# Field products on one core: two eight-pair pieces stored by partition halves, and other cuts in the head's loads

## The reference

```
vid = jnp.einsum('bfd,de->bfe', x, W)
idx_i, idx_j = jnp.triu_indices(32, k=1)
return x[:, idx_i, :] * vid[:, idx_j, :]        # (4096, 496, 64)
```

## Time and profile before

| what | value |
|---|---|
| median of 3 runs | 1284.18 us (1284.15 to 1284.27) |
| the profiled execution | 1284.16 us |
| its span | 1282.8 us |
| PE busy | 189.0 us (15%) |
| DVE busy | 1080.0 us (84%) |
| POOL busy | 0.2 us, 4 instructions |
| DMA moved | 553.70 MB, mean 432 GB/s |

### The profile page before, as it was taken

One profiled execution on the slowest core, in us unless ns is written; L12 is line 12 of the kernel. 1 busy time (PEld: TensorE's weight loads), 2 busy tenths in 40 slices (PEclk: granted clock), 3 DMA queues, 4 the chain that ended last, 5 costly groups with the idle time before them and its releaser, 6 DMA issues. The chain is left out here.

```text
span 1282.8 us, 1256 instructions
## 1 busy us (share of the span) xinstructions
PE 189.0 (15%) x256; PEld 73.3 (6%) x256; DVE 1080.0 (84%) x273; POOL 0.2 (0%) x4
## 2 busy tenths in 40 slices
PE   2012110302112030300020121103030030301100
PEld 1000000100000010100010000001010010100000
DVE  6589989988897989998027989989988899899980
POOL 0000000000000000000000000000000000000000
PEclk8555565655555565655565555656555565655655
DMA  9999999999999999999999999999999999999999
GB/s 403 438 427 430 443 427 433 445 429 425 439 440 429 431 431 440 430 425 445 423 419 438 428 431 438 436 432 432 442 431 436 426 436 435 427 443 433 433 423 409
DMA packets 11810, 553.70 MB, mean 432 GB/s; under 512 B 1312, under 2 KB 1312, under 8 KB 1312
## 3 DMA queue, kind: packets, MB, share of 16 engines
q1 hardware_dynamic: 6048, 277.38, 50.1%
q10 hardware_dynamic: 5760, 276.30, 49.9%
HBM read 33.59 MB, written 520.09 MB: 432 GB/s over the span
## 5 line engine op out<-in xcount | busy, mean ns | idle before, releaser
L296 DVE TENSOR_TENSOR mem<-mem,vid 128x1024 f32<-128x1024 f32 (+11 forms) x270 | 1079.4, 4068 | 161.2 <-DMA out_dram<-mem 113.0
L319 PE MATMUL vid<-mem,w 128*128 x256 | 189.0, 907 | 1005.6 <-PEq L317 1005.6
L319 PEld LDWEIGHTS vid<-mem,w 128*128 128x128 f32 x256 | 73.3, 300 | 1120.5 <-issue 1120.5
L226 DVE COPY w<-mem 64x64 f32<-64x64 f32 x2 | 0.4, 190 | 5.2 <-DMA mem<-in_r_x_dram 5.2
L223 DVE MEMSET w<- 128x128 f32 x1 | 0.2, 165 | 0.8 <-PEq L344 0.8
L344 POOL MEMSET const-bfloat16-1.0<- 128x1 bf16 x1 | 0.1, 101 | 0.0
L344 POOL MEMSET const-uint8-127<- 128x1 uint8 x1 | 0.1, 101 | 0.0
L344 POOL MEMSET const-float32-0.0<- 128x1 f32 x1 | 0.1, 98 | 0.2 <-issue 0.2
L344 POOL MEMSET const-float32-1.0<- 128x1 f32 x1 | 0.1, 98 | 0.0
## 6 DMA issues: line engine op xcount, KB each, us to landing
out_dram<-mem SPq DMA_DIRECT2D x9, 7680.0 KB, 23.3
out_dram<-mem ACTq DMA_DIRECT2D x3, 7680.0 KB, 23.1
out_dram<-mem SPq DMA_DIRECT2D x3, 7168.0 KB, 21.6
out_dram<-mem ACTq DMA_DIRECT2D x3, 5120.0 KB, 17.3
out_dram<-mem ACTq DMA_DIRECT2D x2, 7168.0 KB, 22.6
out_dram<-mem ACTq DMA_DIRECT2D x2, 6656.0 KB, 21.4
out_dram<-mem SPq DMA_DIRECT2D x2, 6656.0 KB, 19.9
out_dram<-mem ACTq DMA_DIRECT2D x3, 4096.0 KB, 17.5
```

The lines of the kernel that those rows point to most:

```text
L226: lambda: nc.vector.tensor_copy(w2[half, half], mem[half, place + F, :D]),
L296: lambda: nc.vector.tensor_tensor(o, left, right, ALU.mult),
L319: last = nc.tensor.matmul(vid[:, b : b + BANK, :], lhsT=w2[:, :], rhs=xt(b), start=True, stop=True)
```

## The change

Four edits. (1) The three pieces of the head's load have 128, 78 and 18 fields in place of 128, 70 and 26. As the first store waits for the piece before the last, it waits for 8 fields more. (2) Slot 1 of 109 pairs becomes two slots of 8 and 101 pairs, and slot 36 of 128 pairs becomes two of 120 and 8. There are now 76 slots, and the switch from ScalarE's to SyncE's queue is at 39, so that it stands between the same pairs. (3) The two slots of 8 pairs, numbers 1 and 38, are stored in two transfers by partition halves. One half of 64 partitions goes from ScalarE's queue as before. The other goes from GpSimd's queue, with an access pattern on the DRAM side whose leading dimension is 8 (8 groups of 8 rows, each group followed by a row's room that is left empty, so that the pattern doesn't merge). For slot 1 GpSimd has partitions 0 to 63, for slot 38 partitions 64 to 127. (4) GpSimd's transfers also wait for the head's last load.

```
-    (0, [(96, 224), (26, 96), (0, 26)]),
+    (0, [(96, 224), (18, 96), (0, 18)]),
...
-STRETCHES = [37]
+STRETCHES = [39]
+SHIFTS = {1: 0, 38: 1}
...
-    (80, 256), (109, 336), (83, 240, 16), ...
+    (80, 256), (8, 336), (101, 344), (83, 240, 16), ...
...
-    (120, 312), (128, 48), (128, 176), (128, 304), (128, 32), (128, 160), (128, 304), (104, 256), (85, 360),
+    (120, 312), (128, 48), (128, 176), (128, 304), (128, 32), (128, 160), (120, 304), (8, 424), (104, 256), (85, 360),
...
+HALVES = P // 2
-BLOCKS = [0, *accumulate(P * row(n) for n, *_ in SLOTS)]
+BLOCKS = [0, *accumulate((P + 8 * (slot in SHIFTS)) * n for slot, (n, *_) in enumerate(SLOTS))]
...
-    sp, act, dve = (Queue(engine, behind) for engine in (nc.sync, nc.scalar, nc.vector))
+    sp, act, dve, pool = (Queue(engine, behind) for engine in (nc.sync, nc.scalar, nc.vector, nc.gpsimd))
...
     hold = load(0)
+    first_loads = hold
...
-        rows = out[BLOCKS[slot] : BLOCKS[slot + 1], :].rearrange("(p u) c -> p u c", p=P)
-        transfer(rows[:, : end - begin, :], mem[:, units[0] : units[1], :], units, True, needs, act if slot < STRETCHES[0] else sp)
+        queue = act if slot < STRETCHES[0] else sp
+        block = out[BLOCKS[slot] : BLOCKS[slot + 1], :]
+        if slot not in SHIFTS:
+            transfer(block.rearrange("(p u) c -> p u c", p=P), mem[:, units[0] : units[1], :], units, True, needs, queue)
+            return
+        apart, size = (HALVES + 8) * (end - begin), end - begin
+        one, other = (slice(h * HALVES, (h + 1) * HALVES) for h in (SHIFTS[slot], 1 - SHIFTS[slot]))
+        groups = block[:apart, :].rearrange("(g p u) c -> g p (u c)", g=8, u=size)[:, :8, :]
+        rest = block[apart:, :].rearrange("(p u) c -> p u c", p=HALVES)
+        transfer(rest, mem[other, units[0] : units[1], :], units, True, needs, queue)
+        transfer(groups, mem[one, units[0] : units[1], :], units, True, [*needs, (first_loads[-1], 16)], pool)
```

More of the change, by code:

```diff
@@ L46 @@
 STARTS = [0, *accumulate(n for n, *_ in SLOTS)]
-def row(n):
-    return n
-BLOCKS = [0, *accumulate(P * row(n) for n, *_ in SLOTS)]
+HALVES = P // 2
+BLOCKS = [0, *accumulate((P + 8 * (slot in SHIFTS)) * n for slot, (n, *_) in enumerate(SLOTS))]
 BREAKS = sorted({a + s for a, (_, _, *seams) in zip(STARTS, SLOTS) for s in seams} | set(STARTS))
@@ L368, with block @@
     got = r.results[0]["out_0_dram"]
-    got = [got[a:b].reshape(P, -1, C)[:, :n] for a, b, (n, *_) in zip(BLOCKS, BLOCKS[1:], SLOTS)]
+    def block(slot):
+        n, rows = SLOTS[slot][0], got[BLOCKS[slot] : BLOCKS[slot + 1]]
+        if slot not in SHIFTS:
+            return rows.reshape(P, n, C)
+        apart = (HALVES + 8) * n
+        both = [rows[:apart].reshape(8, 9, n, C)[:, :8].reshape(HALVES, n, C), rows[apart:].reshape(HALVES, n, C)]
+        return _np.concatenate(both[::-1] if SHIFTS[slot] else both)
+    got = [block(slot) for slot in range(len(SLOTS))]
     got = _np.concatenate(got, axis=1).reshape(2, D, NT, NP, C)
```

## The result

The changed kernel takes 1287.06 us (median of 8 runs, 1286.48 to 1288.78), the kernel before in the same session 1284.22 us (8 runs, 1283.83 to 1284.95). The ratio is 1.0024, with the interval 1.0013 to 1.0035: slower by 2.8 us. I had forecast 1284.5 us, with a range to 1286.4. The profiled execution took 1287.56 us, its span is 1286.2 us, 3.4 us more than before.

A forecast was written before the change was run, and what follows sets the result against it. The prediction took the always busy DMA engines, at 434.5 GB/s, as the bound. It summed 1284.16 + 0.1 + 0.6 - 0.4 + 0 = 1284.46, forecasting 1284.5 us, with a range from 1282.6 to 1286.4 us.

The forecast's parts named there:

- What bounds the kernel: Whole span: DMA engines busy in every slice; 553.70 MB take 1274.3 of 1282.8 us, only 8.5 us can be won.
- The four parts: Losses: 1.7 us before the first packet, 0.4 at 40 us, 1.4 at 638 us, 1.1 from engines ending apart.
- More transfers, +0.1: ScalarE's and GpSimd's queues: four more transfers with 4 KB rows cost 0 to 0.3 us, taken as +0.1.
- The small halves on ScalarE's queue, +0.6: Slots 1 and 38: 64 partitions through 16 engines cost 0 to +0.6 us each, taken as twice 0.3.
- GpSimd's half, "no such loss": Slots 1 and 38: GpSimd's half, one engine for eight partitions as in a whole store, loses no rate.
- The head, -0.4: Change from loads to stores near 40 us: less overlap of directions gains 0 to 0.9 us, taken as -0.4.
- The lag, 0: From about 45 to 604 us one group of eight engines lags by 1.21 us; cost 0, bounds 0 and +1.2.
- half rate: Rival, small halves on ScalarE's queue: +1.2 in place of +0.6, little head gain, 1285.1 us; chance 0.16.
- GpSimd's transfers on all sixteen engines: Rival, GpSimd's halves of slots 1 and 38: spread over all 16 engines, no lag, 1284.3 us; chance 0.05.
- Both on the same eight: Rival, GpSimd's two transfers: the same eight engines get 8 rows more, 1.21 us, 1285.7 us; chance 0.07.
- A preparation of GpSimd's queue: Rival, before the first load or after the last landing: readying or closing the queue costs 2.9 us, 1287.4 us; chance 0.10.
- "Out of step is better": Rival, first half and end: engine groups meet less, gaining 0.5 us and another 0.4, 1283.2 us; chance 0.14.

The follow-up runs named there:

- head alone: The kernel before with only the head's pieces changed to 128, 78 and 18 fields: 1284.78 us, ratio 1.0005.
- head and cuts: The changed kernel with both slots of 8 pairs stored whole from ScalarE's queue, so edits 1 and 2 only: 1285.29 us, ratio 1.0007.
- one cut: The kernel before with slot 1 cut into 8 and 101 pairs, slot 36 whole, all slots stored whole, head as before: 1284.17 us, ratio 1.0000.
- the old head: Head pieces of 128, 70 and 26 fields as before; the changed kernel with them 1287.14 us, the kernel before with both cuts 1284.42 us.
- the big halves: Slot 2 of 101 pairs stored as two 64-partition halves from ScalarE's queue, against the changed kernel, other slots whole: 1301.62 us, ratio 1.0134.
- the twins: Slot 2 from ScalarE's queue on eight engines, 8 neighbouring partitions an engine in two transfers against 4 in four: 1330.84 and 1308.26 us.
- 34 fields: The kernel before with the head's pieces cut to 128, 62 and 34 fields: 1284.54 us, ratio 1.0002.

## Why the prediction was wrong

The time lay outside the range, 2.6 us above the forecast. By the profiles, on the last engine (landings of the store of slot 6, of the store at 622 us, and the end):

| kernel | slot 6's store | at 622 us | end of span | between | rest |
|---|---|---|---|---|---|
| before | 123.1 | 622.2 | 1282.8 | 499.1 | 660.6 |
| head alone | 122.2 | 622.4 | 1283.1 | 500.2 | 660.7 |
| head and cuts | 122.5 | 622.9 | 1284.5 | 500.4 | 661.6 |
| the full change | 125.0 | 625.4 | 1286.2 | 500.4 | 660.8 |

(Slot 6 is that of the kernel before; with slot 1 cut it is number 7.)

The landings of the full change are from these lines:

```profile
L192 ACTq DMA_DIRECT2D out_dram<-mem x1: 339/339/339, 106.9 to 106.9; - x1
DMA to landing us min/median/max: 18.1/18.1/18.1
...
L192 ACTq DMA_DIRECT2D out_dram<-mem x1: 339/339/339, 589.3 to 589.3; - x1
DMA to landing us min/median/max: 36.1/36.1/36.1
```

Its 3.4 us are 1.9 us before 125 us, 1.3 us in the steady stretch, and 0.2 us after it.

- **What bounds the kernel**: right. No slice fell below 9 tenths, and the losses are rate, where engines that are busy move less. The packets keep a mean engine busy 3.5 us longer than before, which is the whole loss in the span (3.4). The four parts that the prediction found of the 8.5 us add up to 4.6 us at most; it left the rest unexplained.
- **The bytes**: right in sum. The page's 553.70 MB are those of before.
- **More transfers, +0.1**: measured +0.1 (one cut) to +0.4 us (both) with the old head, +0.5 with the new, all within what the runs can tell. GpSimd's queue by itself: nothing.
- **The small halves on ScalarE's queue, +0.6**: about right for what their own rows lost. These took 224 and 246 ns in place of 159, which is 0.3 us a half for a mean engine. They did not run at half rate in full, which would be +1.2; the big halves did. That the middle came out was luck: it was taken between two ends with no row for it, and at slot 38 whole rows lose as much beside the loads (241 ns). What the term left out is the big rows beside a half, which lose too.
- **GpSimd's half, "no such loss"**: this step failed. I looked at how many partitions an engine has, eight as in a whole store, and not at which: eight neighbours, where two engines meet on one side, as the twins show at half rate. At slot 38, where it is by itself, GpSimd's half costs a mean engine 0.6 us in the full change and 1.3 with slot 38 alone in halves. All halves together cost 2.1 us of engine time (1.7 us by the medians), where the sum had 0.6.
- **The head, -0.4**: its mechanism was right at its place, and its effect on the time was not. The first store is issued at 39.8 us, the last load lands at 42.5, and with the head alone 0.9 us are won on the last engine and 0.4 in the mean, as reckoned. I took it that a gain there reaches the end; this is the second step that failed. It is gone 500 us later: with the head alone the last engine took 1.1 us more for the same bytes, a mean engine 0.7. The prediction had priced that stretch at "0.1%, 0.5 us", with either sign, and put 0 into the sum.
- **The lag, 0**: its two bounds came true in other kernels. With four halves from ScalarE's queue engines run dry at 166 us, and with both halves from GpSimd's VectorE is released at 78 us. In the changed kernel VectorE was 1.9 us later at 73.84 us, and not 1.2, as the spread grew from 0.9 us (head alone) to 3.2. No engines ran dry in it: its longer span is all packet time. The lag is given back as predicted: the spread falls from 2.6 to 2.1 us while slot 38's GpSimd half goes out, and with slot 38 alone in halves it rises there from 0.9 to 2.2.
- **The rivals**: half rate was right in its mechanism for big slots and did not come in full for the small ones; its 1285.1 us are too low, as it left out GpSimd's half and the steady stretch. (They also hold the head's gain in full, where its text says little.) GpSimd's transfers on all sixteen engines is wrong: in the trace the 64 rows of slot 1's half go out at first eight at a time, 1.7 us apart. Both on the same eight is wrong by the spreads just given. (The sign that the prediction named for it, the spread at the end, tells nothing: it is 0.8 us in the full change and with slot 1 alone in halves.) A preparation of GpSimd's queue was wrong: the whole slots from GpSimd took the time of those from ScalarE. "Out of step is better" had the wrong sign for the whole, and its 1283.2 us don't come out of its terms, 1284.5 - 0.5 - 0.4 = 1283.6.

What stays open is why the long stretches lose more with the new head, with or without halves, and also with the old head when there are halves. From 60 to 606 us these kernels lose 3.8 to 4.2 us (4.7 with both halves from GpSimd's queue), against 2.7 to 3.2 in the kernels with the old head or 34 fields and whole slots. It is no single place: from 123 to 622 us the median row takes 0.6% longer than its bytes in the full change and 0.4% in the kernel before.

My theory was that engines disturb each other when close. The traces speak against it: with 34 fields they are as close at 70 us as with the head alone (1.0 and 0.9 us) and lose least, and in the full change they are 2.5 to 3.2 us apart and lose as much as any. The last engine's 500.4 us in the full change also hold part of GpSimd's half of slot 38, so that row of the table is not quite for the same bytes. Each profile is one execution. Against their own before the halves cost 2.4 us with the old head and 1.7 with the new; that difference is within the noise.

No kernel of these beats the kernel before. The nearest, one cut and the old head, takes the same time.

## What to carry to other kernels

Where all DMA engines are busy all the time, look at which partitions each engine of a transfer reads, not at how many: a transfer of half the partitions, or one whose engines have eight neighbouring partitions, can run at half rate while the engines look busy, and can slow another transfer beside it. How much of it comes depends on how long the rows are and whether the engines meet: in full with rows of 51712 bytes, in part with rows of 4096. What is won at one place on the last engine is no gain until it is seen at the end; here 0.9 us were given back in the next 500. Before trusting a rate in a short window, compare it with a kernel that has the same order of transfers; the time of the packets themselves is the better measure.

## What the runs showed of the hardware

- Sixteen engines on 64 partitions: 207 GB/s at a busy share of 0.97. Eight engines with 8 neighbouring partitions each: a row of 51712 bytes in 4.0 us, 112 GB/s; with 4 neighbours each: 1.9 us.
- The same with rows of 4096 bytes: 214 to 246 ns a row in the mean, between full rate (159) and half, and 165 to 170 at slot 1 with the old head.
- Two transfers on different engines can share the rate: 200 GB/s with all sixteen busy, rows of both at half rate, when one reads partitions 64 to 95; beside a transfer of 0 to 63 the other's rows keep theirs within 4%.
- A transfer from GpSimd's queue with whole slots beside ScalarE's stores costs nothing that can be measured (1285.31 against 1285.29 us). Its rows take turns with the other queue's, one row for one row of 40 to 52 KB: 256 KB take 15.4 us to land, and a second such transfer behind it lands at 78 us.
